# Linear attention and experts in one layer: smaller state products, a group of scores at the end of a round, taps on two engines

## The reference, cut to what matters

```python
xn = layernorm(x)                                  # x: 8 sequences x 2048 tokens x 256
q, k, v = relu(xn @ wq), relu(xn @ wk), xn @ wv    # 16 heads of 16
kv    = cumsum(k[..., :, None] * v[..., None, :])  # over the tokens of a sequence
num   = einsum('bhnd,bhnde->bhne', q, kv)
den   = einsum('bhnd,bhnd->bhn', q, cumsum(k)) + 1e-5
attn  = (num / den) @ wo
# experts: top 2 of 8 by sigmoid(xn @ Wr); four are MLPs (silu(xn @ Wg) * (xn @ Wu)) @ Wd,
# the others multiples of xn, relu(xn) or zero
# a causal convolution of 4 taps along the tokens, per channel
out = x + attn + experts + conv
```

## Time and profile before

| | us |
|---|---|
| median of 3 runs | 1308.19 (1307.94 to 1309.42) |
| the profiled execution | 1308.92 |
| its span, first to last instruction | 1307.1 |
| TensorE busy | 1287.2 (98%) |
| VectorE busy | 1144.3 (88%) |
| GpSimd busy | 830.8 (64%) |
| ScalarE busy | 707.8 (54%) |

### The profile page before, as it was taken

The page is one execution under the profiler, slowest core; times in us unless marked ns, Lnnn a source line. Parts: engine busy times, 40 slices in busy tenths (PEclk is TensorE's granted clock), DMA queues, the critical chain, the costliest instruction groups (busy, mean ns, idle before and its releaser), DMA issues.

```text
span 1307.1 us, 55818 instructions
## 1 busy us (share of the span) xinstructions
PE 1287.2 (98%) x24160; PEld 1116.5 (85%) x24160; DVE 1144.3 (88%) x2686; ACT 707.8 (54%) x1487; POOL 830.8 (64%) x673
## 2 busy tenths in 40 slices
PE   5999999999999999999999999999999999999998
PEld 4888888888888888888888888888888888888887
DVE  7988898888898888988888988889888889888885
ACT  5645655455654456554555544565545555445552
POOL 2676665765666756657656667566576566675554
PEclk9999999999999999999999999999999999999999
DMA  5012212222222222222222222221222222222211
GB/s 185 14 56 73 78 50 51 80 78 78 65 61 56 79 78 79 51 51 81 78 79 64 67 51 78 78 78 51 51 80 78 79 64 67 51 78 63 61 35 34
DMA packets 175860, 88.54 MB, mean 68 GB/s; under 512 B 135552, under 2 KB 171264, under 8 KB 171520
## 3 DMA queue, kind: packets, MB, share of 16 engines
q1 hardware_dynamic: 174912, 83.97, 22.6%
q10 hardware_dynamic: 704, 1.01, 0.2%
HBM read 53.18 MB, written 17.04 MB: 54 GB/s over the span
## 4 chain that ended last, share of the span: by engine, by line
PE 95%; DVE 3%; POOL 1%; issue 1%; ACT 0%; DMA 0%; DVEq 0%; POOLq 0%
PE ring L343 51%; PE scores L343 17%; PE ring L466 7%; PE ring L482 6%; PE scores L415 5%; PE state_sum L429 4%; PE ring L488 2%; PE scores L397 2%; DVE sm L895 1%; POOL xn L731 0%; DMA x_t<-in_L_attn_x_dram 0%; PE scores L352 0%; POOL rstd L722 0%; DVE stats L819 0%; POOL x_t L748 0%
## 5 line engine op out<-in xcount | busy, mean ns | idle before, releaser
L757 POOL TENSOR_TENSOR hid<-hid,cwb 128x512 f32<-128x512 f32 x128 | 166.4, 1300 | 181.8 <-DVE hid L924 181.0
L916 DVE SCALAR_TENSOR_TENSOR cT<-xT,conv_ws,cT 128x512 f32<-128x512 f32 x192 | 275.1, 1471 | 0.0
L745 POOL TENSOR_TENSOR x_t<-x_t,same 128x1024 f32<-128x1024 f32 x32 | 76.9, 2404 | 254.9 <-ACT same L618 254.9
L639 ACT ACTIVATE sg<-ring 128x512 f32<-128x512 f32 x128 | 76.6, 599 | 268.5 <-PE ring L343 268.5
L343 PE MATMUL ring<-xl,wgu_h 128*128 128x512 f32 x512 | 213.1, 416 | 0.0
L761 POOL TENSOR_TENSOR hl<-hid,hh 128x512 fp32r<-128x512 f32 x128 | 208.8, 1632 | 0.0
L343 PE MATMUL ring<-xh,wgu_l 128*128 128x512 f32 x512 | 201.0, 393 | 0.3 <-issue 0.3
L343 PE MATMUL ring<-xh,wgu_h 128*128 128x512 f32 x512 | 200.5, 392 | 0.0
L569 ACT ACTIVATE yh<-yT 128x256 fp32r<-128x256 f32 x128 | 53.5, 418 | 246.7 <-DVE yT L933 246.7
L902 DVE TENSOR_TENSOR state_bd<-state_sum,tables_s 128x256 f32<-128x256 f32 x248 | 104.0, 419 | 93.8 <-PE state_sum L429 90.6
L895 DVE TENSOR_TENSOR sm<-scores,causal_s 128x512 f32<-128x512 f32 x256 | 157.7, 675 | 6.0 <-PE scores L415 5.0
(11 more groups left out here) (134 smaller groups left out, 3453.4 us busy)
## 6 DMA issues: line engine op xcount, KB each, us to landing
cwb<-cw_rows SPq DMA_DIRECT2D x32, 1024.0 KB, 4.6
x_t<-in_L_attn_x_dram SPq DMA_DIRECT2D x32, 512.0 KB, 4.2
out_dram<-x_t SPq DMA_DIRECT2D x31, 512.0 KB, 2.9
xT<-qks_tok SPq DMA_DIRECT2D x896, 16.0 KB, 1.8
cw_rows<-cwt SPq DMA_DIRECT2D x128, 2.0 KB, 1.4
sm<-in_L_attn_wqkv_dram ACTq DMA_DIRECT2D x2, 384.0 KB, 5.0
sm<-in_L_ffn_Wg_dram SPq DMA_DIRECT2D x2, 256.0 KB, 3.8
sm<-in_L_ffn_Wu_dram SPq DMA_DIRECT2D x2, 256.0 KB, 4.6
```

The lines of the kernel that those rows point to most:

```text
L639: act.activation(sg[:, :], GB[t % 2], ACT.Silu).then_inc(s_sg, 1)
L745: pool.tensor_tensor(xb, xb, same[:, :, :], ALU.add).then_inc(s_base1, 1)
L757: pool.tensor_tensor(hid[:, e, :], hid[:, e, :], cwb[:, e, :], ALU.mult).then_inc(s_hid, 1)
L916: ins = dve.scalar_tensor_tensor(out=cT[:, c, :], in0=xT[:, third(s, j, 0), c, LEAD - HALO + n:LEAD - HALO + n + BT], scalar=conv_ws[:, c, ...
```

## The change

Five edits.

State times query: `state_bd` (256 columns, block diagonal) becomes `state_ph` (64 columns); `blocks` multiplies the sum by the parity of the head alone, and each product takes the 32 rows and 32 columns of one pair of heads. Sixteen products a tile in place of eight.

The scores of tiles 2 and 3 of a batch move from behind tile 0's numerators to the end of the round before, behind the fourth output tile (`scores(s, j, 1, 1)`); for the first batch they follow its first state sum. They wait for the mask of the scores ahead of them. Their mask moves to the end of VectorE's round as well.

Taps 1 to 3, from the fourth round on and except in the last: ScalarE writes the scaled x into the banks SB[0] and SB[1] (`tap_terms`), and VectorE adds it (`add_terms`). The key products wait for the last addition.

FILL goes.

```diff
-    FILL = 38
-        state_bd = sb("state_bd", [P, 4, D])
+        state_ph = sb("state_ph", [P, 4, C, BLK])
+        TB = SB[0:2]
...
+                if k and by_blocks(s, j, k):
+                    pe.wait_ge(s_conv, at(s, j, HALO, HALO))
                 for g in range(C):
                     project(KB[g][:, :], D + g * P).then_inc(s_kp, 1)
...
                 if u:
-                    pe.wait_ge(s_sm, at(s, j, U * ROWS, ROWS))
+                    pe.wait_ge(s_sm, at(s, j, U * ROWS, k * U * ROWS + ROWS))
...
-                            for w in range(2):
-                                rows = slice(w * HALF, (w + 1) * HALF)
-                                cols = slice(g * P + w * HALF, g * P + (w + 1) * HALF)
-                                ins = mm(NB2[t % 2][h][rows, g * HALF:(g + 1) * HALF], state_bd[:, n % 4, cols],
-                                         qT[:, g, n0:n0 + HALF], start=False, stop=True, skip_group_check=True)
+                            for m in range(PPG):
+                                rows = slice(BLK * m, BLK * m + BLK)
+                                ins = mm(NB2[t % 2][h][rows, g * HALF:(g + 1) * HALF], state_ph[rows, n % 4, g, :],
+                                         qT[rows, g, n0:n0 + HALF], start=False, stop=True, skip_group_check=True)
...
-                if not last and by_blocks(s, j, 1):
-                    for _ in range(FILL):
-                        pe.wait_ge(tables_in, 16)
                 for t in range(T):
                     gate_up(t)
                     numerators(t)
-                    if t == 0:
-                        scores(s, j, 0, 1)
...
                     output(t)
+                scores(s, j, 1, 1)
...
+                def tap_terms(n):
+                    if n == 1:
+                        act.wait_ge(s_sm, at(s, j, U * ROWS, U * ROWS))
+                    else:
+                        act.wait_ge(s_conv, at(s, j, HALO, n - 1))
+                    for c in range(C):
+                        first = LEAD - HALO + n
+                        ins = act.activation(TB[c][:, :], xT[:, third(s, j, 0), c, first:first + BT], ACT.Copy,
+                                             scale=conv_ws[:, c, n:n + 1])
+                    ins.then_inc(s_tapped, 1)
...
                 high_hid(0)
+                if ahead:
+                    tap_terms(1)
...
-                dve.tensor_tensor(state_bd[:, n % 4, :].rearrange("p (g m n) -> p g m n", g=C, m=PPG),
-                                  ST.unsqueeze(2).to_broadcast([P, C, PPG, BLK]),
-                                  same_head_s[:, :].rearrange("p (m n) -> p m n", m=PPG).unsqueeze(1)
-                                  .to_broadcast([P, C, PPG, BLK]), ALU.mult).then_inc(s_bd, 1)
+                dve.tensor_tensor(state_ph[:, n % 4, :, :].rearrange("p g (a d) -> p g a d", a=2),
+                                  ST.rearrange("p g (a d) -> p g a d", a=2),
+                                  parity_s[:, :].unsqueeze(1).unsqueeze(3).to_broadcast([P, C, 2, HD]), ALU.mult
+                                  ).then_inc(s_bd, 1)
...
+                def add_terms(n):
+                    ...
+                    dve.wait_ge(s_tapped, (s * BPS + j - BY_PE + 1) * HALO + n)
+                    for c in range(C):
+                        ins = dve.tensor_tensor(cT[:, c, :], TB[c][:, :], cT[:, c, :], ALU.add)
+                    ins.then_inc(s_conv, 1)
...
                         if left > 1 and by_blocks(s, j, 2):
                             turn_x(s, j, 2)
-                        mask(s, j, 0, 1)
...
                     dve.tensor_tensor(xb, done[:, 0:D], xb, ALU.add).then_inc(s_out, 1)
+                if not last:
+                    mask(s, j, 1, 1)
```

More of the change, by code:

```diff
@@ L225, in layer_kernel @@
         s_conv = sem("s_conv")
+        s_tapped = sem("s_tapped")
         s_op = sem("s_op")
@@ L563, in _ @@
             state_sum(0, 0, 0, 0)
+            scores(0, 0, 0, 1)
             pe.wait_ge(w_split, N_SPLITS)
@@ L679, in batch @@
                 high_hid(1)
+                if ahead:
+                    tap_terms(2)
                 high_y(2)
@@ L682, in batch @@
                 high_hid(2)
+                if ahead:
+                    tap_terms(3)
                 high_y(3)
@@ L901, in blocks @@
                 dve.wait_ge(s_st, chunk_at(s, j + k, n))
-                dve.tensor_tensor(state_bd[:, n % 4, :].rearrange("p (g m n) -> p g m n", g=C, m=PPG),
-                                  ST.unsqueeze(2).to_broadcast([P, C, PPG, BLK]),
-                                  same_head_s[:, :].rearrange("p (m n) -> p m n", m=PPG).unsqueeze(1)
-                                  .to_broadcast([P, C, PPG, BLK]), ALU.mult).then_inc(s_bd, 1)
+                dve.tensor_tensor(state_ph[:, n % 4, :, :].rearrange("p g (a d) -> p g a d", a=2),
+                                  ST.rearrange("p g (a d) -> p g a d", a=2),
+                                  parity_s[:, :].unsqueeze(1).unsqueeze(3).to_broadcast([P, C, 2, HD]), ALU.mult
+                                  ).then_inc(s_bd, 1)
             def batch(s, j, left):
                 last = left == 0
+                def add_terms(n):
+                    if n == 1:
+                        dve.wait_ge(s_tap0, at(s, j, 1, 1))
+                    else:
+                        dve.wait_ge(s_conv, at(s, j, HALO, n - 1))
+                    dve.wait_ge(s_tapped, (s * BPS + j - BY_PE + 1) * HALO + n)
+                    for c in range(C):
+                        ins = dve.tensor_tensor(cT[:, c, :], TB[c][:, :], cT[:, c, :], ALU.add)
+                    ins.then_inc(s_conv, 1)
                 def tap(n):
+                    if not last and by_blocks(s, j, 1):
+                        add_terms(n)
+                        return
                     if n == 1:
@@ L1020, in _ @@
             mask(0, 0, 0, 0)
+            mask(0, 0, 0, 1)
             blocks(0, 0, 0, 1)
```

## The result

The changed kernel takes 1341.3 us (median; 1337.2 to 1343.5), the kernel before 1308.5 beside it: ratio 1.0247, interval 1.022 to 1.0273, so slower by 33 us. Forecast were 1326, with a range from 1306 to 1339. The profiled execution of the changed kernel took 1340.5 us, with a span of 1338.7, 31.6 above that of before.

A forecast was written before the change was run, and what follows sets the result against it. TensorE, busy 1287.2 of 1307.1 us, was taken as the bound. Terms of +2.0 us of TensorE and +16.1 us of waits made +18.1, on 1308.2 giving 1326 us, range 1306 to 1339.

The forecast's parts named there:

- state products: State times query on TensorE: sixteen 32 by 32 products start slightly earlier, -0.014 us a tile, -1.8 us in all.
- `blocks`: VectorE's masking of the state gets shorter, so the second state sum follows the numerators directly: -5.8 us, bounds 0 and -9.6.
- taps: Scalings on ScalarE and additions on VectorE, some 1.6 us per tap moved, off TensorE's path: costed at nothing.
- change of shape: Moved scores break a run of full-array products behind the fourth output tile: +0.16 us a round, +5.0 in all.
- start-up: First scores to move wait for the first mask: +4.1 us; `blocks` queued behind mask and `statistics` at second round's end: +0.5.
- waits for the mask: Moved scores wait on TensorE for VectorE's mask, late through the turned-x transfers: +16.1 us, bounds 5.5 and 31.
- FILL: 38 waits per round run in TensorE's sequencer while its queue is full; removing them gains nothing.
- The chain from transfers to mask to scores: Scores wait for VectorE's mask, reached only through `products`, which waits for 32 transfers; start at transfers' length + 9.20 us.
- its threshold: Moved scores wait in every round whose 32 transfers take above 23.17 us: 22 of the 28 lengths.
- the overlap of the 32 by 32 products: On TensorE four run side by side, one per quadrant: again eight groups of 0.058 us.
- rival (3): State products: the four row tiles take turns on the PSUM bank, +178 us, about 1490 us; chance 0.04.
- Rival (4): TensorE's waits of 1 to 2 us cost clock too: some ten long waits, 2 us each, about 1345 us; chance 0.07.

The follow-up runs named there:

- e7: The kernel before with the taps alone in the changed form (scaled on ScalarE, added on VectorE): 1308.7 us, ratio 0.9997.
- e5: The changed kernel with 64 by 64 state products, two pairs of heads each, in place of its own: 1320.6 us, ratio 1.0086.
- e6: The kernel before with the 32 by 32 state products alone and the 38 FILL waits kept: 1330.4 us, ratio 1.0167.
- e12: The kernel before with the move of the scores and without the FILL waits, state products and taps as before: 1330.9 us, ratio 1.0174.
- e2: The kernel before with its 38 FILL waits removed and nothing else: 1318.2 us, ratio 1.0072.
- s1: The kernel before, FILL kept, with 120 waits (60 instructions) added at the very start, where TensorE is idle: 1333.9 us, ratio 1.0186.
- e3: The changed kernel with the turned x tile in a memory of its own, so `products` waits for no transfer: 1338.4 us, ratio 1.024.
- e1: The changed kernel without its move: the last two tiles' scores and their mask back in the next round's first tile: 1326.2 us, ratio 1.0138.
- e10: The kernel before with the move of the scores and their mask alone, FILL kept: 1388.0 us, ratio 1.0621.
- e4: The kernel before with state times query as 64 by 64 products of two pairs of heads, nothing else changed: 1300.9 us, ratio 0.994.

## Why the prediction was right and wrong

| step | predicted, us | in the changed kernel's profile |
|---|---|---|
| state products | -1.8 | -3.5 |
| `blocks` | -5.8 (0 to -9.6) | -7.6 |
| taps | 0 | 0 (e7) |
| change of shape | +5.0 | +4.5 (2.0 + 2.5) |
| start-up | +4.1 and +0.5 | +5.0 and 0 |
| waits for the mask | +16.1 (5.5 to 31) | +17.2 |
| FILL, and some 124 new instructions a round | 0 | +16 (14.6 stops, 1.5 clock) |
| sum | +18.1 | +31.6 |

**Right.** The chain from transfers to mask to scores, its threshold and its size. The transfers are over 23.17 us in 17 of 28 rounds now, not in 22, by 15.4 us in all; the waits sum to 17.2. That the size fits so well is partly luck: the prediction took the lengths of the kernel before, and they change with TensorE's stream (in e5, with the same chain, 12 of 28 are over 23.17 us, by 5.5 us in all). Right were also the gate by `blocks`, the taps, and the overlap of the 32 by 32 products: first to last record 0.435 us instead of 0.463, so that rival (3) is out. The Trainium skill (TensorEngine Tiling (Array Packing), Restrictions and Gotchas) says that different row tiles cannot access one bank at the same time. The trace differs: four of them, each writing partitions of its own, wrote one bank and the group got no longer.

The start-up came out at +5.0 against 4.1. TensorE waits 4.12 us for the first mask, and then scores and gate products run at the lower clock (timeline of after, the granted clock behind the wait, 0.50, which is 1.2 GHz, then the same gate product of before):

```profile
33.78 2.01 PE L419 MATMUL scores<-qp,kT 32*64 32x128 f32 x64 [4.12 <-DVE sm L912]
...
41.34 0.50 PE L344 MATMUL ring<-xl,wgu_h 128*128 128x512 f32 x1
```

```profile
33.80:38.40 4.60, 4.60 (x70) 3.74 (x71) 2.50 (x5) 0.00 (x0) 0.00 (x0) 0.50 0.00 0
```

```profile
36.34 0.50 PE L343 MATMUL ring<-xl,wgu_h 128*128 128x512 f32 x1
```

**Wrong: the step on the state products, -1.8 us, which counted their time and not their number, and with it the step on FILL, "Removing them gains nothing", costed at 0.** Their time came out about as forecast. But the state products lengthen a tile's run of small instructions from 224 to 256, a whole block, and in the changed kernel 14.6 us of stops and 1.5 us of lower clock follow, which the sum didn't have. By themselves, with FILL kept, they cost 21 us (e6); with 64 by 64 products FILL is missing just the same and one stop is left (e5), and so it is with the old products (e12). The prediction also saw that FILL takes no time and concluded that it does nothing. In the kernel before it sets the length of a round in instructions, and so where block boundaries lie (e2: 9.5 us; s1: 25 us for a shift alone); what the changed kernel would take with its own rounds padded to whole blocks was not run. The row that would have told was on the page of before: 191 packets of the instruction queue, 3.13 MB, for 49,080 TensorE instructions. The prediction never asked what some 124 more a round meant.

How a block comes to be late shows when packets and block boundaries are paired in order (the first packet with the second boundary). At 2521 block boundaries in the thirteen traces TensorE never passes one sooner than 2.17 us after the start of that block's packet, and in all 115 stops of over 0.25 us it goes on 2.17 to 3.19 us after it (535.42 to 538.35 in the one above). The packet itself starts between 4.2 us before and 5.3 us after TensorE passes the boundary before, at the median 0.77 us after. So a stop is what is left of these times when TensorE is through the block in hand sooner, and a run of 256 small instructions is: from 534.85 to 536.51 in that timeline, 1.7 us. In e3 the four longest stops (2.0 to 2.7 us) follow packets that started 1.6 to 5.1 us after their boundary; for the same blocks of the changed kernel it is 0.3 to 4.1 us. Why a packet starts when it does, and why later in e3, stays open.

The Trainium skill (Runtime: NRT & Kernel Launch, Instruction fetch mechanics) describes the blocks of 256 and the fetching ahead, which these packets agree with. It also calls the fetch hidden by the pace of issue. The stops in e1, e2, e6 and s1 show that in runs of small products it is not.

**Rival (4)**, long standstills that cost clock as well, happened once behind the start-up, not some ten times, and behind a stop, not behind a wait for the mask; that its 1345 us lie near the measured time is chance. After the stop of 1.72 us that ends at 1150.52 (columns as in the stretch of e10 above):

```profile
1140.00:1150.00 10.00, 8.79 (x257) 7.26 (x242) 7.07 (x15) 3.14 (x6) 5.34 (x7) 1.00 0.41 136
1150.00:1155.00 5.00, 4.49 (x25) 3.54 (x25) 1.76 (x5) 1.90 (x4) 3.06 (x3) 0.66 0.07 13
```

A clock of 0.66 over 5 us is 1.7 us lost; behind the start-up, the other stops and waits of this run, up to 1.70 us long, left it at 1.00. The length alone doesn't decide: a stop of 2.08 us in e3 (to 331.58) left it at 1.00 too.

## What to carry to other kernels

Cost an edit in instructions as well as in microseconds: on an engine that issues runs of small products, count how many stand in a row and where the blocks of the instruction queue begin, and shorten the step without adding instructions if you can (e4: 7.8 us won with fewer elements and the same count). A loop of waits that takes no time may still hold the stream in place, and it can cost time once the work that stands ahead of it is short (1.6 us a round in e10). A step moved behind a chain that has no slack pays whenever that chain is late (here in 18 rounds and at the start).

## What was not expected of the hardware

Sixty instructions (120 waits) in the idle start of the kernel cost 25 us later on (s1), by nothing but the places of 256-instruction blocks. FILL's 38 waits cost nothing behind the output products of before, some 1.6 us in each of 28 rounds behind 64 short records (e10), and save 9.5 us where they were (e2). And four row tiles wrote one bank side by side with no loss (32 records in 0.65 us, 16 before in 0.69).
